# Two-layer attention block on one core: row maxima begin after four q/k projections, the other four stand among them

## The reference

```python
x = x + attn0(layernorm(x), Wq, bq, Wk, bk, Wv, bv, Wo, bo)   # scores/4 + slope[h]*(key - 1023), causal, softmax
x = x + ffn0(layernorm(x))     # silu(x Wg) * (x Wu), then Wd; W = (wq - 128) * scale, hidden 704
x = x + attn1(layernorm(x), Wq, Wk, Wv, Wo)                   # scores/4, causal, softmax
x = x + ffn1(layernorm(x))     # weights rounded to fp8 e4m3, scales per output channel, hidden 768
```

## Time and profile before

| | us |
|---|---|
| median of 3 runs (lowest to highest) | 449.85 (447.51 to 450.31) |
| the profiled execution | 446.99 |
| its span from first to last instruction | 445.3 |

### The profile page before, as it was taken

One profiled execution on the slowest core, in us unless ns is written; L12 is line 12 of the kernel. 1 busy time (PEld: TensorE's weight loads), 2 busy tenths in 40 slices (PEclk: granted clock), 3 DMA queues, 4 the chain that ended last, 5 costly groups with the idle time before them and its releaser, 6 DMA issues.

```text
span 445.3 us, 14589 instructions
## 1 busy us (share of the span) xinstructions
PE 397.3 (89%) x6360; PEld 205.2 (46%) x6360; DVE 310.2 (70%) x630; ACT 244.2 (55%) x361; POOL 178.3 (40%) x255
## 2 busy tenths in 40 slices
PE   5898988999998888999799998888999988888997
PEld 4355743343334237544367555433333342365476
DVE  7865889999997116521744558999999971178883
ACT  3433556678788963221100442666887879735950
POOL 8416022403214134478682000234362553453770
PEclk9998989999999989999999999999999999999999
DMA  6069200000000000200100242100000000000002
GB/s 202 30 209 283 67 30 4 4 4 4 4 3 5 2 2 16 68 3 10 62 0 0 79 140 82 64 3 6 3 3 5 1 5 2 1 2 0 2 24 72
DMA packets 14889, 16.77 MB, mean 38 GB/s; under 512 B 1868, under 2 KB 14090, under 8 KB 14826
## 3 DMA queue, kind: packets, MB, share of 16 engines
q1 hardware_dynamic: 13730, 12.83, 9.1%
q0 software_dynamic: 544, 2.49, 1.8%
q10 hardware_dynamic: 552, 0.53, 0.4%
HBM read 8.27 MB, written 1.05 MB: 21 GB/s over the span
## 4 chain that ended last, share of the span: by engine, by line
PE 50%; DVE 24%; ACT 9%; POOL 8%; issue 5%; DMA 3%; SPq 1%; ACTq 0%; DVEq 0%; POOLq 0%
DVE mx L1327 17%; PE ps L846 10%; ACT prob L1210 8%; PE ps L792 7%; PE ps L1008 4%; PE ps L983 4%; PE ps L1044 4%; PE ps L1088 4%; PE ps L830 3%; PE ps L723 3%; PE ps L907 3%; PE ps L978 2%; DMA kS<-alibi_tail 2%; POOL oT L595 1%; POOL prob L632 1%
## 5 line engine op out<-in xcount | busy, mean ns | idle before, releaser
L1327 DVE TENSOR_REDUCE mx<-ps 128x1 f32<-128x512 f32 (+3 forms) x320 | 181.4, 628 | 27.3 <-PE ps L802 23.8
L1210 ACT ACTIVATE prob<-ps,s_exp 128x1024 f32<-128x1024 f32 (+1 forms) x192 | 163.3, 900 | 54.7 <-PE ps L830 53.9
L632 POOL TENSOR_SCALAR_AFFINE_SELECT prob<-prob 128x256 f32<-128x256 f32 x128 | 52.1, 411 | 168.3 <-ACT prob L1210 167.8
L792 PE MATMUL ps<-kS,qS 64*32 64x512 f16 (+11 forms) x1536 | 102.1, 321 | 15.7 <-DVE mx L1327 10.2
L846 PE MATMUL ps<-prob,v 128*32 128x512 f32 (+3 forms) x768 | 83.6, 507 | 2.0 <-POOL prob L632 1.4
L830 PE MATMUL ps<-qS,kS 64*32 64x512 f16 (+3 forms) x1528 | 76.8, 329 | 7.4 <-ACT prob L1210 6.6
L792 PEld LDWEIGHTS ps<-kS,qS 64*32 64x32 f16 x1536 | 35.5, 89 | 94.9 <-DVE mx L1327 80.5
L798 PE MATMUL ps<-mask_q,identb 64*32 64x32 bf16 (+1 forms) x1024 | 46.8, 180 | 0.0
L802 PE MATMUL ps<-mask_q,identb 64*32 64x64 bf16 (+1 forms) x512 | 41.6, 194 | 0.0
L830 PEld LDWEIGHTS ps<-qS,kS 64*32 64x32 f16 x1528 | 29.6, 90 | 24.1 <-ACT prob L1210 18.1
L978 PE MATMUL ps<-xnT,gu0T 128*128 128x512 f32 x80 | 34.9, 593 | 0.0
(11 more groups left out here) (156 smaller groups left out, 549.4 us busy)
## 6 DMA issues: line engine op xcount, KB each, us to landing
qS<-parts SPq DMA_DIRECT2D x24, 128.0 KB, 2.1
kS<-parts SPq DMA_DIRECT2D x24, 128.0 KB, 2.2
out<-x SPq DMA_DIRECT2D x8, 128.0 KB, 1.7
oT<-in_L_ffn_gate_w POOLq DMA_DIRECT2D x1, 768.0 KB, 4.9
oT<-in_L_ffn_up_w POOLq DMA_DIRECT2D x1, 768.0 KB, 4.7
parts<-in_L_ffn_down_w POOLq DMA_DIRECT2D x1, 768.0 KB, 5.5
prob<-in_L_ffn_wq_down SPq DMA_DIRECT2D x1, 704.0 KB, 6.2
prob<-in_L_ffn_wq_gate SPq DMA_DIRECT2D x1, 640.0 KB, 4.6
```

The source lines that it names most:

```text
L632: nc.gpsimd.affine_select(out=square, in_=square, compare_op=ALU.is_ge, fill=0.0, base=0, pattern=[[0, 2], [1, P]], channel_multiplier=-1) ...
L792: mmi = nc.tensor.matmul(span[r:r + STRIP, 0:seen], qS[own, c, pair, qt * P + r:qt * P + r + STRIP], kS[own, pair, key0:key0 + seen], star ...
L1210: nc.scalar.activation(prob[:, n % 3, pair::G // 2, off:CH], ps[:, 2 * (m % 2):2 * (m % 2) + 2, off:CH], ACT.Exp, scale=s_exp[:, L:L + 1]) ...
L1327: ins = nc.vector.tensor_reduce(mx[:, slot, qt, us[0]:us[-1] + 1, part], src, AX_X, ALU.max)
```

## The change

1. `QK_JOBS` is a new table, and only its first four projections (`QK_EARLY` = 4: q and k of head half 0, chunk 0, then chunk 1) stand ahead of the attention. The other four, and in layer 0 the bias product, become `late` entries of `ORDER`, placed by `LATE_AT` behind a number of maximum or turn entries; DVE takes their low part (`lo`) three entries later. They use PSUM bank 7.
2. All side jobs are placed by a table `SIDES_AT`; none stands ahead of the first maximum. ACT takes side jobs and late projections in the order of the list.
3. `CGS` puts (2, 0) second to last, so the last two cgs are small ones. `ORDER` is one list for each layer; in layer 0 `FIRST_TURN_AHEAD` is 33 in place of 7, so 48 entries stand ahead of the first exp step there. `W8_DOWN_AT` stays 3.
4. The memsets of `qS` and `kS` are gone. Two DMAs of 512 KB, issued behind Wv and Wo, fill the shared rows: `kS` from `alibi_tail`, which now holds all 32 of them, `qS` with zeros. Of the six small DMAs two stay (`alibi_q`). The low-part code of DVE waits after each instruction instead of working on two projections at a time.
5. PE makes the product of `w_top` (L1052) behind the first projection instead of ahead of it.

```diff
+QK_JOBS = ((0, 0, 0), (0, 0, 1), (0, 1, 0), (0, 1, 1), (1, 0, 1), (1, 1, 0), (1, 1, 1), (1, 0, 0))
+QK_EARLY = 4
+LATE = (tuple(range(QK_EARLY, N_QK)) + ("bias",), tuple(range(QK_EARLY, N_QK)))
...
-CGS = [(0, 0), (1, 0), (2, 0), (0, 1), (1, 1), (2, 1), (3, 1), (3, 0)]
+CGS = [(0, 0), (1, 0), (0, 1), (1, 1), (2, 1), (3, 1), (2, 0), (3, 0)]
...
-FIRST_TURN_AHEAD = 7
+FIRST_TURN_AHEAD = (33, 7)
...
+LATE_AT = ((2, 7, 12, 17, 22), (1, 6, 11, 16))
+LO_BEHIND = 3
+SIDES_AT = ((1, 1, 4, 4, 6, 6, 9, 9, 24, 24, 27, 27, 30, 30, 33, 33, 36, 36, 39, 39, 42), (3, 3, 8, 8, 13, 13, 18, 18))
...
+            nothing = rows_of[2 * HD:2 * HD + 1, :, 0:CH]
+            sp.dma_start(k_chunks[0:P:ROW_STEP], rows_of[0:2 * HD, :, 0:CH]).then_inc(tail_in, 16)
+            sp.dma_start(q_chunks[0:P:ROW_STEP], nothing.to_broadcast([2 * HD, NH // 2 * NC, CH])).then_inc(q_clear, 16)
...
-                            sp.dma_start(k_chunks[alibi_rows(half)], rows_of[half, 0:ALIBI_ROWS, :, 0:CH]).then_inc(tail_in, 16)
                             sp.dma_start(q_chunks[alibi_rows(half)], alibi_q[half * HALF:half * HALF + ALIBI_ROWS * NH // 2 * NC]).then_inc(tail_in, 16)
-                            sp.dma_start(k_chunks[half * HALF:(half + 1) * HALF:HALF // MAX_ROWS],
-                                         rows_of[half, ALIBI_ROWS:ALIBI_ROWS + MAX_ROWS, :, 0:CH]).then_inc(tail_in, 16)
...
-            nc.gpsimd.memset(q_words[:, 1], 0.0).then_inc(stack_zero, 1)
...
-            nc.gpsimd.memset(k_flat.bitcast(F32), 0.0).then_inc(stack_zero, 1)
...
+            def late_job(L, job):
+
+                if job == LATE[L][0]:
+                    pe.wait_ge(b_free, B_AT["on", L, RING[0]])
+                else:
+                    pe.wait_ge(late_free, late_made(L, job) - 1)
...
+                    projection_qk(L, job, bank).then_inc(late_full, 1)
...
+            def second_part(L, n, bank, free):
...
+                if L == 0:
+                    chain(nc.vector.tensor_scalar(rest[:, n % 2], bank, s_qk[:, L, w:w + 1], bqk_s[:, w, mt:mt + 1], ALU.mult, ALU.add))
+                    settle()
+                    nc.vector.engine_nop().then_inc(free, 1)
+                    nc.vector.tensor_tensor(parts[:, n, 1], rest[:, n % 2], parts[:, n, 0], ALU.subtract).then_inc(lo_done, 1)
...
-            nc.vector.memset(q_words[:, 0], 0.0).then_inc(stack_zero, 1)
```

248 lines of the change are left out of this document (126 added, 122 removed).

## The result

The changed kernel takes 478.19 us (median of 4 runs, 476.07 to 478.46) against 449.58 us before: 1.063 times as long, 95% interval 1.059 to 1.068. The direction of the forecast was right; its size, 459 us with a range up to 467, was not. The profiled execution has a span of 476.7 us, 31.4 more than that of before, and a mean granted clock of 0.953 (before 0.987).

The account below looks back on a forecast made before the run. DVE's rate was taken to bound the maxima, ACT's exponentials each layer's end. 446.99 + 3.5 (layer 0) - 0.5 (layer 1's start) + 7.2 (stall) = 457.2, or 460.1 shifted to the median; forecast 459 us, range 449.5 to 467.

Parts of the forecast that it names:

- 3.6 of the 8.9 fit: +5.3: Layer 1's start: of 8.9 us more PE work among the first 22 entries 3.6 fit, costing 5.3 us.
- 3 x 0.8, +2.4: Layer 1's start: each late projection but the first waits 0.8 us for bank 7, costing 2.4 us.
- Layer 0's +3.5: All of layer 0: -7.5 + 6.5 + 2 + 2 + 1 - 0.5 = +3.5 us (-2 to +8).
- layer 0, first maximum: Start of layer 0: first maximum at 29.6 instead of 37.05, -7.5 us (-9.8 to -5).
- two small cgs behind it: Layer 0, only 20 entries beside them: DVE needs 12.4 us, ACT 14, costing +2 us (0 to 4).
- layer 1, first maximum: Start of layer 1: first maximum behind the fourth projection, at about 255.5 instead of 264.16, -8.7 us.
- DVE 6.5, PE 18 us in the first 12 entries: Layer 0's maxima: low parts and bias sum cost DVE +6.5 us; PE's 18 us leaves DVE idle, +2.
- Rival (a): Both layers' starts: PE has room for what moved, so 447.5 us, no change; chance 0.14.
- The stall: Middle of layer 1: PE waits for POOL's cut behind its rounding and DVE's mask, +7.2 us (6.2 to 8).
- Rival (b): Each layer's end: small cgs shorten the tail if ACT keeps up with the maxima, 442.2 us; chance 0.07.
- (c): Both layers' starts: the earlier starts come through whole, moved work hidden in DVE's idle time, 438 us; chance 0.05.
- (d): Slower still: alibi DMAs land late as before (+2.5), ACT cannot catch up in layer 0 (+4), 466 us; chance 0.12.

Follow-up runs that it names:

- fill_alone: The kernel before with the shared rows filled by DMA instead of the three memsets, nothing else: 441.9 us, 0.985.
- mask_early: The changed kernel with DVE's mask of the down weights at the turn of cg 2 instead of cg 3: 468.8 us, 1.045.
- cgs_alone: The kernel before with the changed order of the cgs and the mask at the turn of cg 2: 446.7 us, 0.998.
- cgs_and_fill: The kernel before with the changed order of the cgs, the mask at cg 2 and the DMA fill instead of the memsets: 442.0 us, 0.984.

## Why the prediction was wrong in size

The three steps that made the forecast "slower" stood: layer 0 loses, layer 1's start gains nothing, POOL's rounding stalls layer 1. What failed are the sizes of terms: the sum was +10.2 us, the traces show +31.4. The step that failed most plainly is the price of the late projections at layer 1's start, "3.6 of the 8.9 fit: +5.3" and the hand-over of bank 7, "3 x 0.8, +2.4": they measured 7.9 and 4.8. Layer 0's +3.5 measured +13.7, because its first maximum, its late work and its small cgs were each priced about 3 us too low. In the profiled executions the difference grows to 13.7 us at the last exponential of layer 0, 15.4 ahead of layer 1's transposes, 20.8 at its first exponential, 31.4 at the end. Term by term (us):

| term | forecast | measured |
|---|---|---|
| layer 0, first maximum | -7.5 | -4.4 |
| first maximum to first exponential | 44.4 long | 47.7 long |
| two small cgs behind it | 14 long | 16.9 long |
| three large cgs | 51.7 long | 52.5 long |
| layer 0 in all | +3.5 | +13.7 |
| between the layers | 0 | +1.7 |
| layer 1, first maximum | -8.7 | -7.3 |
| to the first exponential | +7.7 | +12.7 |
| order of the cgs and stall | +0.5 + 7.2 | +10.6 |

- **The start.** The memset's wait went as said, but I had the projection ahead of the scales cost nothing more than its length. It brought a wait of 2.61 us on DVE; fill_alone, without it, has its scales at 11.87. The first maximum also had scatter: the same program put it at 30.96 in mask_early. The issues ended at 27.3 instead of 25.2, and the rows landed 5.4 us behind that where I had 4.4, which is within the bounds of the landing. By the Trainium skill (DMA: Bandwidth & Descriptors, "Why a DMA increments its semaphore by 16 and not by 1"), which gives a transfer only as many engines as divide its outer dimension, I estimated a landing near 29.5, and the rows landed at 32.7; no run here tells how many engines they had. And the early start is not the moved work's: the fill alone brings 3.6 us of it, the projections 1.3.
- **Late work in layer 0.** "DVE 6.5, PE 18 us in the first 12 entries" was priced by the busy time of each engine; the chain from PE over ACT to DVE and back over one bank was left at 1 us. The four projections alone cost 10.7 us between first maximum and first exponential, where the sum had 6.5 + 2 for all that moved; DVE was idle 14 us there, not 9, though the stretch as a whole was only 3.3 us too long. With the low part one entry sooner it is 44.9 us (mask_early 47.6), so the hand-over has a part in layer 0 too. POOL's conversion, which I expected beside the moved low parts, had ended at 39.7, and the first of them began at 42.7; all eight took 0.69 us. (49 entries stand ahead of the first exponential, not 48; this changes nothing in the sum.) Rival (a), that PE has room, fell with it: the 35 us of waiting lay where no hand-over stood.
- **The small cgs.** Missed by the clock: 79 to 88 us ran at half clock, 16.9 us instead of 14; the same cgs took 14.73 us at 0.94. The three large ones behind them were 0.8 us over the forecast. The sum had taken the clock as full behind the first entries.
- **Between the layers.** Forecast at nothing, it took 1.7 us more: a stretch at half clock (0.98 here, 1.00 before), of which the last section has more.
- **Layer 1's start.** Of the -8.7 the four projections brought their 6.9; the new order of jobs adds one wait of 1.08 us for ACT's copy of the second half. The forecast let 3.6 us of the moved work fit, since it counted PE as needed for 11.2 of 14.8 us; the row of before has PE busy 12.90 of 14.81. With only one wait for bank 7 left the stretch took 22.7 us, 7.9 more than before where I had 5.3. The hand-over, 3 x 0.8 = 2.4, measured 4.8: PE waited four times, 5.1 us in all. The low part was thought to stand behind a maximum of 0.6, and stood behind two side jobs of 1.99 in PE's order.
- **The stall.** Its place, its chain and its 8.5 us on PE were as said. Forecast at 7.2, it measured 8.3 in the traces and 9.4 by the medians. The other 2.3 of the +10.6 stay when it is gone (112.0 us of exponentials in mask_early, 109.7 before). cgs_alone, which has the new order and no stall, shows nearly the same, 111.6. There the order of the cgs, forecast at +0.5, goes with a lower clock (the third number from the end); here is the stretch in cgs_alone, and then before:

```profile
278.37:389.97 111.60, 99.91 (x2392) 39.67 (x2393) 87.05 (x169) 84.34 (x103) 45.98 (x83) 0.95 0.03 8
```

```profile
278.97:388.64 109.67, 97.21 (x2392) 37.98 (x2385) 86.20 (x169) 84.40 (x103) 45.90 (x83) 1.00 0.03 8
```

- **The tail.** Rival (b), the small cgs shorten the tail, would have been cgs_alone at 442 to 445; it measured 446.7. But its mechanism is there in layer 0: without the third small cg the stretch ahead of the large ones is 7.8 us shorter in cgs_alone than before, and the tail, with it, 5.4 longer. All exponentials take 109.3 us and 111.6 before, 109.1 in cgs_and_fill and 111.7 in fill_alone. The 2.3 to 2.6 us are lost again at lower clocks, 1.6 to 1.7 between the layers (0.98 and 1.00) and 1.4 to 1.9 in layer 1's exponentials (0.95 and 1.00). The forecast had -0.5 for layer 0's tail.
- **The other rivals.** (c) holds for the fill alone, 441.9, and for nothing that moved. (d), slower still, came nearest to what happened: the rows landed 3.1 us later than forecast (it had 2.5), and the late first exponential is one of the things that an edit gave back. It had 466 (its terms add up to 463.7) and nothing of the hand-over or the clock.

Of the 28.6 us that the change costs, the edits gave back 9.4 at POOL, 13.6 at layer 0's projections, 3.1 at its first exponential, 3.4 at its side jobs, 2.6 at the scales and 4.6 at layer 1's projections (3.3 by the traces); from this goes what the fill brings, 5. This is 3 us too much: the parts overlap, and most of them hold a share of falls of the clock, which is not taken apart.

## What to carry to other kernels

Price work that is moved by its ring of hand-overs, not by engine busy time: follow the buffer from the engine that fills it to the one that frees it, and count everything that stands in each engine's order between the two, side jobs too. Before moving work behind a start, look whether the start waits for something else: where PE is idle 8 us for a transfer, 7 us of work ahead of it cost 1.3. And time the parts of a combined change one by one: here one part, alone, makes the kernel 1.5% faster.
